# A last layer of sixteen tiles in another order: recurrence adds first in a tile, first product two tiles ahead, second one tile behind

## The reference, cut to what matters

```python
def step(state, inp):                     # over the 128 time steps, 16 sequences x 64 states
    d_t, p_t = inp
    state = jax.nn.silu(d_t + state) + p_t
    return (state, state)
...
h = h + states @ out_w.T + out_b          # the product with out_w is "outp"
...
gate = fp4_linear(x, w_gate)              # x = layernorm(h), 2048 x 256;, w_gate, w_up: 704 x 256
y = fp4_linear(x, w_up)
h2 = jax.nn.silu(gate) * y
out = h + fp4_linear(h2, w_down)          # 704 -> 256
```

## Time and profile before

| what | us |
|---|---|
| median of 3 runs | 648.58 (646.12 to 651.47) |
| profiled execution, its time | 644.06 |
| profiled execution, span | 642.0 |
| around the span | 2.06 |
| first recurrence step | 441.3 |
| busy over the span: TensorE 86%, VectorE 70%, ScalarE 38%, GpSimd 20% | |

### The profile page before, as it was taken

How to read it: one execution, slowest core, us unless ns; L and a number is a source line. 1 busy time by engine, 2 the same in 40 slices (tenths; PEclk the granted TensorE clock), 3 DMA queues, 4 the chain that set the end, 5 groups by cost and what they waited for, 6 DMA issues and landing times.

```text
span 642.0 us, 9655 instructions
## 1 busy us (share of the span) xinstructions
PE 550.5 (86%) x3260; PEld 347.4 (54%) x3260; DVE 448.0 (70%) x1207; ACT 246.7 (38%) x776; POOL 131.6 (20%) x244
## 2 busy tenths in 40 slices
PE   2788989989989998998998998993658898989894
PEld 2554556566466565665565656742325555555553
DVE  1365655875786686687587586384579999999852
ACT  1362254156146136326316415703334444443321
POOL 6407511001001100110110100001222424243210
PEclk9998999999999998999999998897579999999997
DMA  7701100000000000000000000003300000000000
GB/s 189 245 3 41 30 13 2 0 1 0 0 0 0 0 0 0 0 0 0 0 0 0 0 0 1 2 1 71 59 2 8 17 10 16 10 16 9 18 17 16
DMA packets 13518, 12.77 MB, mean 20 GB/s; under 512 B 2795, under 2 KB 12724, under 8 KB 13492
## 3 DMA queue, kind: packets, MB, share of 16 engines
q1 hardware_dynamic: 12212, 10.34, 6.1%
q0 software_dynamic: 1280, 2.11, 1.2%
HBM read 8.25 MB, written 2.10 MB: 16 GB/s over the span
## 4 chain that ended last, share of the span: by engine, by line
PE 47%; DVE 21%; POOL 9%; issue 9%; ACT 7%; SPq 4%; DMA 2%; POOLq 0%; DVEq 0%; ACTq 0%
PE psum L601 18%; ACT probs L924 5%; PE psum L541 5%; PE psum L632 4%; POOL hq L462 3%; SPq L366 3%; POOL rstd L410 3%; PE psum L677 2%; PE psum L520 2%; DVE stats L1214 2%; PE psum L646 2%; PE psum L545 2%; DVE neg_max L1236 2%; DVE hsc L1154 2%; DVE wgu_tmp L1164 2%
## 5 line engine op out<-in xcount | busy, mean ns | idle before, releaser
L601 PE MATMUL psum<-expw_sb,n2T 128*128 128x512 f32 x256 | 118.1, 605 | 0.0
L407 POOL TENSOR_TENSOR rstd<-meanvar,ln_eps_col 128x1 f32<-128x1 f32 x64 | 15.8, 246 | 348.6 <-DVE meanvar L1218 348.5
L845 PE MATMUL psum<-wguT,n2T 128*128 128x512 f32 (+1 forms) x192 | 82.7, 582 | 0.0
L924 ACT ACTIVATE probs<-psum,neg_max 128x128 f32<-128x128 f32 x256 | 68.6, 399 | 26.2 <-DVE neg_max L1236 26.2
L601 PEld LDWEIGHTS psum<-expw_sb,n2T 128*128 128x128 f32 x256 | 46.7, 193 | 47.0 <-issue 47.0
L867 PE MATMUL psum<-wdT,probsT 128*128 128x256 f32 x192 | 49.7, 402 | 16.1 <-ACT probsT L893 16.1
L1236 DVE TENSOR_REDUCE neg_max<-psum 128x4 f32<-128x512 f32 x64 | 40.5, 685 | 27.7 <-PE psum L545 27.6
L1067 ACT ACTIVATE probs<-u_now 64x16 f32<-64x16 f32 x128 | 27.6, 216 | 83.2 <-DVE u_now L1446 83.0
L845 PEld LDWEIGHTS psum<-wguT,n2T 128*128 128x128 f32 x192 | 38.0, 199 | 39.5 <-issue 34.3
L867 PEld LDWEIGHTS psum<-wdT,probsT 128*128 128x128 f32 x192 | 34.7, 194 | 29.1 <-issue 23.9
L893 ACT ACTIVATE probsT<-psum 128x512 f32<-128x512 f32 x72 | 36.9, 527 | 30.6 <-PE psum L555 26.1
(11 more groups left out here) (157 smaller groups left out, 947.3 us busy)
## 6 DMA issues: line engine op xcount, KB each, us to landing
expw_sb<-in_expert_w SPq DMA_DIRECT2D x8, 256.0 KB
expw_sb<-hidden SPq DMA_DIRECT2D x16, 128.0 KB
result<-res SPq DMA_DIRECT2D x16, 128.0 KB
w_raw<-in_w_down SPq DMA_DIRECT2D x1, 704.0 KB, 9.1
w_raw<-in_w_gate SPq DMA_DIRECT2D x1, 640.0 KB, 7.0
w_raw<-in_w_up SPq DMA_DIRECT2D x1, 640.0 KB, 8.0
wexp_sb<-in_w_expand SPq DMA_DIRECT2D x1, 256.0 KB, 3.0
wproj_sb<-in_w_project SPq DMA_DIRECT2D x1, 256.0 KB, 3.2
```

Of the source, the lines that this page charges most:

```text
L601: last = mm(pq[:, g, :], n2T[:, u, k, :], expw_sb[:, k, EPQ * g:EPQ * (g + 1), :].rearrange("p e n -> p (e n)"), start=(k == 0), stop=(k = ...
L845: last = mm(pgu[u][:, c0:c1], xqT[:, u, k, :], wguT[:, k, c0:c1], start=(k == 0), stop=(k == KD - 1))
L924: last = nc.scalar.activation(probs[:, u, h, :], pq[:, g, j * T:(j + 1) * T], ACT.Exp, bias=neg_max[:, u, h:h + 1])
```

## The change

Nothing is computed otherwise; instructions move. The core of the diff:

```diff
+TURNED_ALONE = 5
-        turned = sems("turned", 3)
+        turned = sems("turned", TURNED_ALONE + 1)
...
             states(1)
+            x_rescaled(0)
             rstd_of(3, 1, 2)
-            x_rescaled(0)
...
-                wait(pe, xqT_ready, j - 2 if j > 3 else j - 1)
+                wait(pe, xqT_ready, j - 1)
...
-                pe.wait_ge(h4_done, min(j + 3, TILES) if j > 1 else j + 2)
+                pe.wait_ge(h4_done, min(j + 2, TILES))
...
+            def gate_up(j, banks):
+                for c in banks:
+                    if c == banks[0]:
+                        pe.wait_ge(xqT_ready, j + 1)
+                    if c < 2:
+                        wait(pe, hqT_ready[c], j - 1)
...
+            gate_up(1, (0, 1, 2))
+            x_transposed(2)
+            outp(4)
             for j in range(TILES):
-                if j + 4 < TILES:
-                    outp(j + 4)
-                if j + 1 < TILES:
-                    gate_up(j + 1)
-                if j + 2 < TILES:
-                    x_transposed(j + 2)
-                h_transposed(j)
-                down(j)
+                h_transposed(j)
+                if j + 2 < TILES:
+                    gate_up(j + 2, (2, 0))
+                if j + 3 < TILES:
+                    x_transposed(j + 3)
+                if j + 2 < TILES:
+                    gate_up(j + 2, (1,))
+                if j + 5 < TILES:
+                    outp(j + 5)
+                if j > 0:
+                    down(j - 1)
+            down(TILES - 1)
...
             for j in range(TILES):
                 beside = steps_beside(j)
-                gated_beside(beside[0:3])
-                h_sizes(j)
-                gated_beside(beside[3:4])
-                if j + 3 < TILES:
-                    x_sizes(j + 3)
-                gated_beside(beside[4:8])
-                if j + 1 < TILES:
-                    silu(j + 1)
-                if j + 2 < TILES:
-                    x_transposed(j + 2)
-                h_transposed(j)
+                if j > 0:
+                    h_transposed(j - 1)
+                gated_beside(beside[0:2])
+                if j + 2 < TILES:
+                    x_transposed(j + 2)
+                gated_beside(beside[2:5])
+                h_sizes(j)
+                gated_beside(beside[5:6])
+                if j + 3 < TILES:
+                    x_sizes(j + 3)
+                gated_beside(beside[6:8])
+                if j + 1 < TILES:
+                    silu(j + 1)
+            h_transposed(TILES - 1)
```

On VectorE ahead of the loop 13 adds stand before `add_outp(0)` (11 before), all 40 before `h_product(0)` (37 before), and fewer of them between the steps of x. `add_outp(j)` waits for its own transfer up to j = 4, and `add_outp(5)` for all that are left. In the loop (`third`: tile j+3 exists, `fourth`: tile j+4 exists) VectorE's order becomes this:

```diff
+                h_fp4(0, j)
+                advance_beside(0)
+                    x_fp4(0, j + 3)
+                advance_beside(1)
+                h_fp4(1, j)
+                h_fp4(2, j)
+                advance_beside(2)
+                    x_fp4(1, j + 3)
+                h_fp4(3, j)
+                advance_beside(3)
+                    x_fp4(2, j + 3)
+                advance_beside(4)
+                h_fp4(4, j)
+                advance_beside(5)
+                    x_fp4(3, j + 3)
+                    x_fp4(4, j + 3)
+                advance_beside(6)
+                h_fp4(6, j)
+                advance_beside(7)
+                h_fp4(7, j)
+                    add_outp(j + 4)
+                    x_stats(j + 4)
+                    x_aggregate(j + 4)
+                    x_fp4(6, j + 3)
+                    x_fp4(7, j + 3)
+                if j > 1:
+                    result(j - 2)
+                    x_norm(j + 4)
+                    h_product(j + 1)
```

More of the change, by code:

```diff
@@ L365, in _ @@
             for j in range(TILES):
-                sp.dma_start(by_time[:, j, :], hidden[STEPS * j:STEPS * (j + 1), :, :]).then_inc(turned[min(j, 2)], 16)
+                sp.dma_start(by_time[:, j, :], hidden[STEPS * j:STEPS * (j + 1), :, :]).then_inc(turned[min(j, TURNED_ALONE)], 16)
             for j in range(TILES):
@@ L846, in gate_up @@
                                   start=(k == 0), stop=(k == KD - 1))
-                last.then_inc(gu_done, 1)
+                if 1 in banks:
+                    last.then_inc(gu_done, 1)
             def h_transposed(j):
@@ L874, in _ @@
             outp(2)
-            gate_up(0)
+            gate_up(0, (0, 1, 2))
             x_transposed(1)
             outp(3)
+            gate_up(1, (0, 1, 2))
+            x_transposed(2)
+            outp(4)
             for j in range(TILES):
-                if j + 4 < TILES:
-                    outp(j + 4)
-                if j + 1 < TILES:
-                    gate_up(j + 1)
+                h_transposed(j)
                 if j + 2 < TILES:
-                    x_transposed(j + 2)
-                h_transposed(j)
-                down(j)
+                    gate_up(j + 2, (2, 0))
[8 more added lines that the diff above has]
+            down(TILES - 1)
         @block.scalar
@@ L1108, in _ @@
             x_transposed(0)
-            for t in range(25, 29):
-                gated(t)
+            gated(25)
+            gated(26)
             x_sizes(1)
-            for t in range(29, 37):
+            for t in range(27, 34):
                 gated(t)
             x_sizes(2)
+            for t in range(34, AHEAD):
+                gated(t)
             silu(0)
             x_transposed(1)
-            for t in range(37, AHEAD + 1):
-                gated(t)
+            gated(AHEAD)
             for j in range(TILES):
                 beside = steps_beside(j)
-                gated_beside(beside[0:3])
+                if j > 0:
[4 more added lines that the diff above has]
+                gated_beside(beside[2:5])
                 h_sizes(j)
-                gated_beside(beside[3:4])
+                gated_beside(beside[5:6])
                 if j + 3 < TILES:
                     x_sizes(j + 3)
-                gated_beside(beside[4:8])
+                gated_beside(beside[6:8])
                 if j + 1 < TILES:
                     silu(j + 1)
-                if j + 2 < TILES:
-                    x_transposed(j + 2)
-                h_transposed(j)
+            h_transposed(TILES - 1)
         @block.vector
@@ L1449, in add_outp @@
                 dve.wait_ge(outp_done, j + 1)
-                if j <= 2:
-                    dve.wait_ge(turned[j], 16 * (TILES - 2) if j == 2 else 16)
+                if j < TURNED_ALONE:
+                    dve.wait_ge(turned[j], 16)
+                elif j == TURNED_ALONE:
+                    dve.wait_ge(turned[j], 16 * (TILES - TURNED_ALONE))
                 V.tensor_tensor(by_time[:, j, :], poutp, by_time[:, j, :], ALU.add).then_inc(h4_done, 1)
@@ L1486, in result @@
                 V.tensor_tensor(res[:, j % 2, :], pdown, by_time[:, j, :], ALU.add).then_inc(res_ready, 1)
-            for t in range(11):
+            for t in range(13):
                 advance(t)
             add_outp(0)
-            advance(11)
+            advance(13)
             x_stats(0)
-            advance(12)
+            advance(14)
             x_aggregate(0)
-            advance(13)
-            advance(14)
+            advance(15)
+            advance(16)
             x_norm(0)
-            for k in range(5):
-                x_fp4(k, 0)
-                advance(15 + k)
@@ L1501, in _ @@
[L1501 to L1527, removed]
+            ahead = iter(range(17, AHEAD))
+            def advance_next():
+                for t in ahead:
+                    advance(t)
+                    break
+            for m in range(3):
+                x_fp4(0, m)
+                advance_next()
+                x_fp4(1, m)
+                x_fp4(2, m)
+                advance_next()
+                x_fp4(3, m)
+                x_fp4(4, m)
+                advance_next()
+                if m < 2:
+                    add_outp(m + 1)
+                    advance_next()
+                x_fp4(6, m)
+                if m < 2:
+                    x_stats(m + 1)
+                x_fp4(7, m)
+                advance_next()
+                if m < 2:
+                    x_aggregate(m + 1)
+                    advance_next()
+                    advance_next()
+                    x_norm(m + 1)
@@ L1528, in _ @@
+            for t in ahead:
+                advance(t)
             h_product(0)
             add_outp(3)
-            advance(37)
-            x_fp4(6, 2)
             x_stats(3)
-            advance(38)
-            x_fp4(7, 2)
             x_aggregate(3)
-            advance(39)
             x_norm(3)
@@ L1586, in _ @@
                     h_product(j + 1)
+            result(TILES - 2)
             result(TILES - 1)
```

18 lines of the change are left out of this document (removed).

## The result

The changed kernel's median is 655.35 us (653.11 to 663.45, 4 runs) against 648.73 (646.12 to 651.47, 4 runs). The ratio is 1.0087, 95% interval 1.0045 to 1.0129 (the highest of the four, a slow execution, is not in it). Measured again in more rounds it was 1.0113 (1.0084 to 1.0141). The forecast was 653.6 us and "within 1%". The measured cost is about 1%: the first ratio lies inside that, the repeat's just outside.

What follows compares the result with a forecast made beforehand. VectorE's loop was taken as the longer one after the change, 10.72 us a tile. +5.8 up to h_product(11) and -0.8 at the end gave +5.0 on the median of 648.58: 653.6 us, range 645 to 661.

Steps and rivals of the forecast that it cites:

- (a) to (e): VectorE's steady tile, h_product to next h_product, in five parts: 3.66 + 2.00 + 0.91 + 3.60 + 0.55 = 10.72 us, +0.35 a tile.
- (d): h_fp4(7) to x_norm: 3.60 us against 3.68, with add_outp and statistics beside GpSimd's rescaling and x_fp4(6) waiting for GpSimd.
- x_stats beside the rescaling: Between h_fp4(7) and x_norm: x_stats, 0.42 us, runs while GpSimd rescales without being held, at a cost of 0.
- rival 3: x_stats is held by GpSimd's rescaling: +5 us more, 658.6 us; chance 0.10.
- Both loops close at the same time: Steady tile before the change: VectorE's and TensorE's loops both take 10.37 us, TensorE's being 9.25 of work plus 1.12 idle.
- Start, -1.5: Up to h_product(1): add_outp(2)'s transfer wait goes, h_fp4(0, 0) moves -2.6, a late copy adds +0.75; h_product(1) comes 1.5 us sooner.
- the +0.75 for the late copy: Tile 0: the copy of x of tile 2 waits on ScalarE for gate_up(1), ahead of Silu 43, costing 0.75 us.
- Clock in tiles 1 and 2, +3.8: Idle TensorE falls to the low clock before h_transposed(0) and (1), making x's copies and Silus late: 1.9 us a tile.
- Rival 1: The clock doesn't fall in tiles 1 and 2, so 3.8 us is gone: +1.2, 649.8 us; chance 0.17.
- Rival 4: TensorE's idle 1.5 us drops the clock in the steady part too: +12 us more over some eight tiles, about 666; chance 0.05.
- End, -3.3 and +2.5: h_product(11) to h_transposed(15) 3.3 us shorter; from there to result's end 2.5 longer, as down(14) precedes down(15); net -0.8.
- Rival 2: TensorE's loop alone is the bound and the adds cost nothing: every tile 9.25 us, -13.5 in all, 635.1; chance 0.10.

Runs made afterwards that it cites:

- e5: Kernel before with only the recurrence adds and Silus moved to the change's places, five adds ahead of h_fp4(4); ratio 1.0059, 10.89 us a tile.
- e8: Kernel before with only add_outp, x_stats and x_aggregate moved behind h_fp4(7), beside GpSimd's rescaling; ratio 0.9976, 10.08 us a tile.
- e1: Changed kernel with the loop's recurrence adds and Silus back where they stood before; ratio 0.9906 to the kernel before, tiles 3 to 10 at 10.03 us.
- e2_fill: Changed kernel with products of constants added on TensorE ahead of h_transposed(0) and h_transposed(1); ratio 1.0057 to the kernel before.
- e7: Changed kernel with e2_fill's added products and two more ahead of h_transposed in each of tiles 2 to 10; ratio 1.0025 to the kernel before.

## Why the prediction was right, point by point

**The tile, (a) to (e): right.** 10.60 came for 10.72, and each part lies within 0.07 of its term: 3.60 (3.66), 1.93 (2.00; its terms add up to 1.96, not the 1.97 written), 0.91 (0.91), 3.61 (3.60), 0.55 (0.55). In (d) x_norm starts 2.64 after the rescaling's start, as in the earlier trace rows, though x_fp4(6) takes 0.81 and not 1.43, for it starts later and ends with the same release. e5 and e8 show that the 0.23 is the sum of +0.52 for the adds and -0.29 for add_outp and x_stats. The step from the rows to "the adds behind the rescaling lie in a wait that stays" is shown by e1: put back there, the three cost 0.08, the price I gave, and 0.67 goes ahead of h_fp4(4) (2.93 against 3.60).

**x_stats beside the rescaling: right,** 0.43, so rival 3 falls.

**"Both loops close at the same time": wrong.** I read TensorE's 1.12 of waiting as part of a second loop that was as tight as VectorE's. In e8 the tile falls to 10.08 and the wait to 0.83 with TensorE's order untouched. It was slack. This didn't enter the sum, as VectorE's loop was taken to be the longer one after the change. It would have spoiled a forecast for e8.

**Start, -1.5: wrong in size and sign, +0.25.** The transfer wait did go, and h_product(0) came at 24.92 after the first add, against 26.29. Two terms failed. h_fp4(0, 0) was to come 2.6 sooner; it came 1.90 sooner (29.02 against 30.92 after the first add), as add_outp(3) ahead of it waited 0.72 for outp(3). And from there to h_product(1) it took 11.63 where my terms make 10.56, because the +0.75 for the late copy had gate_up(1) at the high clock. Behind 3.80 of idle time outp(3) took 1.19 and gate_up(1) 6.05, x's copy and everything behind it on ScalarE was late, and VectorE stood idle 1.82. In e2_fill gate_up(1) took 1.63 longer still, and h_product(1) came 1.64 later. The late copy costs this only behind the adds placed first: h_product(0) to (1) is 15.73 here and 14.10 in e1, where gate_up(1) was as slow (6.58).

**Clock in tiles 1 and 2, +3.8 beside the tile's own +0.35 each: right,** +4.3 in all against +4.5. e2 shows the cause. Rival 1 falls.

**Rival 4 had a part in it.** I gave it 0.05 and priced it for every tile. A clock under 1.00 in the steady part was one of my signs of being wrong, and it came, in one tile of eight: +1.55, the price I gave for a late copy, once. The tiles with 1.12 of idle time have none, nor has e7 with 0.49.

**End, -3.3 and +2.5: right,** -3.46 and +3.11. Most of the 0.6 missing is down(15)'s wait of 0.52 for result(14), which I left out (and my terms add up to 9.27, not 9.2): both products go to one PSUM tile, and VectorE has to read it in between.

**Sum.** +5.0 forecast, +7.5 in the profiled stage, 1.0087 and 1.0113 in the timed runs (5.6 and 7.3 us). What I missed is the start (1.75), tile 7 (1.4) and the two terms of the end (0.45 net), less 1.1 for the other tiles. The misses are 3.6 one way and 1.1 the other, on a forecast of 5.0. The steady tile, tiles 1 and 2 and the end were forecast for the right reasons; that the total came no farther off, with the start's sign wrong and tile 7 left to a small chance, is in part luck. Rival 2, the faster one, fell: h_products came no closer than 10.59 while there were adds beside them, and TensorE's idle time moved and didn't go.

## What to carry to other kernels

An engine's instructions may stand in a wait on another engine for nothing, and in front of the bounding chain at full price: find out which of an engine's idle pieces stays after the change, and leave the short chained work in it. A chain of small steps across two engines (0.45 us a step here) must be priced by its round trip, not by the 0.17 that each step is busy. And work that is pulled ahead on TensorE leaves idle time elsewhere, where its clock can fall, as it did here in tiles 0 and 1 after 5.11 and 4.20 us. Try parts of a reordering alone, since here two of them were worth 1.1% and the others took back 2%.

## What the runs showed of the hardware that was not expected

The clock fell in the steady part with idle pieces of 1.56 us in tiles of 10.6: once among eight equal tiles, in the same tile 7, in three profiled executions, twice in a fourth (e2_fill, tiles 3 and 8), and not at all in nine whose longest piece in a tile lay between 0.49 (e7) and 1.13 (before). In e5_adds_early two pieces of 0.86 and 0.56 in each tile, 1.42 together, didn't bring it down.

The part of the program ahead of the stage, which no kernel here touches, took 441.6 to 449.1 us to the first recurrence add in the profiled executions, a spread of 7.5 us, as much as the whole effect of the change on its stage. The stage itself repeated to 0.1 us for the same kernel (204.8 and 204.8, 187.3 and 187.3). But its start can vary as well: h_product(0) came 26.29, 26.30 (e5) and 25.22 (e8) after the first add with the same code up to there, and h_product(0) to (1) took 17.37 in e2_fill and 15.78 in e7_fill_all. For changes of about 1% a stage measured off in the timeline told more than the total, the steady tiles above all. What makes the first part vary was not tried.
